# Moments of nine chunks made early, the experts' square moved to ScalarE, and one tile map made in two parts, in a perceiver block on one core

## The reference, cut to what matters

```python
x = x + xattn(layernorm(x), ctx_1024, ...)       # 64 sequences of 32 tokens, 257 context rows each, D = 256
# x + attn(layernorm(x), ...): time mixing, then a mixture of 8 experts
probs = jax.nn.softmax(ei @ router_w, axis=-1)
vals, idx = jax.lax.top_k(probs, 2)
tw = jnp.sum(jax.nn.one_hot(idx, E) * (vals / vals.sum(-1, keepdims=True))[..., None], axis=-2)
k_e = jnp.square(jax.nn.relu(jnp.einsum('ebsd,edf->ebsf', xk_e, eWk)))   # F = 512
kv_e = jnp.einsum('ebsf,efd->ebsd', k_e, eWv)
r_e = jax.nn.sigmoid(jnp.einsum('ebsd,edg->ebsg', xr_e, eWr))
moe = jnp.einsum('ebsd,bse->bsd', r_e * kv_e, tw)
# x + ffn(layernorm(x), ...): a shared GEGLU and one of 8 GEGLU experts for each token
```

## Time and profile before

| | |
|---|---|
| median of 3 runs | 944.83 us (944.8 to 945.19) |
| the profiled execution | 948.37 us, span 946.3 us |
| PE busy | 863.0 us, 91% of the span |
| DVE busy | 457.3 us, 48% |
| ACT busy | 316.4 us, 33% |
| POOL busy | 342.7 us, 36% |

### The profile page before, as it was taken

How to read it: one execution, slowest core, us unless ns; L and a number is a source line. 1 busy time by engine, 2 the same in 40 slices (tenths; PEclk the granted TensorE clock), 3 DMA queues, 4 the chain that set the end, 5 groups by cost and what they waited for, 6 DMA issues and landing times.

```text
span 946.3 us, 18950 instructions
## 1 busy us (share of the span) xinstructions
PE 863.0 (91%) x6360; PEld 774.4 (82%) x6360; DVE 457.3 (48%) x1355; ACT 316.4 (33%) x714; POOL 342.7 (36%) x580
## 2 busy tenths in 40 slices
PE   5899988887767789999967999999999999999998
PEld 4567767665666679999957999999999999999998
DVE  1269988889873565555535666621111111111114
ACT  1366767665453334444421111111111111111110
POOL 1444677775876336654313333010001100000033
PEclk9899999998589889999997999999999999999999
DMA  9775457435512222253311122065898989998114
GB/s 353 262 265 211 162 161 246 124 118 207 167 40 63 52 63 84 82 174 126 79 42 54 57 67 68 12 245 207 322 318 304 308 325 318 306 323 288 56 52 134
DMA packets 92110, 162.00 MB, mean 171 GB/s; under 512 B 13832, under 2 KB 71112, under 8 KB 88680
## 3 DMA queue, kind: packets, MB, share of 16 engines
q1 hardware_dynamic: 71008, 103.39, 32.6%
q10 hardware_dynamic: 12832, 37.82, 10.6%
q0 software_dynamic: 8176, 19.57, 7.8%
HBM read 146.10 MB, written 14.66 MB: 170 GB/s over the span
## 4 chain that ended last, share of the span: by engine, by line
PE 65%; DVE 13%; POOL 6%; DVEq 6%; issue 5%; DMA 3%; ACT 1%; ACTq 1%; another core or an unknown queue 0%; SPq 0%; POOLq 0%
PE bank L1635 27%; PE bank L1648 14%; PE bank L372 7%; PE bank L399 7%; PE bank L386 3%; DMA xz<-in_x_dram 2%; DVEq L1388 2%; PE bank L361 1%; DVE arena_b L1191 1%; POOL tab_e L685 1%; PE bank L779 1%; DVE arena_b L1211 1%; DMA arena_a<-rows_y,slot 1%; PE bank L1618 1%; DVE arena_b L501 0%
## 5 line engine op out<-in xcount | busy, mean ns | idle before, releaser
L1635 PEld LDWEIGHTS bank<-arena_b,arena_a 128*128 128x128 f32 x1472 | 168.0, 192 | 1.2
L1635 PE MATMUL bank<-arena_b,arena_a 128*128 128x128 f32 x1472 | 168.1, 275 | 0.0
L1701 ACT ACTIVATE arena_b<-bank 128x512 f32<-128x512 f32 x78 | 46.6, 597 | 301.0 <-PE bank L1635 301.0
L1843 DVE TENSOR_TENSOR arena_b<-bank,arena_b 128x512 f32<-128x512 f32 x78 | 54.0, 692 | 190.8 <-PE bank L1635 186.0
L1635 PE MATMUL bank<-arena_b,a_x 128*128 128x128 f32 x1024 | 122.6, 280 | 0.0
L1635 PEld LDWEIGHTS bank<-arena_b,a_x 128*128 128x128 f32 x1024 | 119.6, 196 | 0.4
L328 POOL DMA_INDIRECT arena_a<-rows_e,pick x78 | 76.0, 975 | 29.5 <-issue 29.5
L372 PE MATMUL bank<-arena_b,arena_a 128*128 128x128 f32 x624 | 82.2, 289 | 4.2 <-DVE hT L509 4.2
L1648 PE MATMUL bank<-arena_a,arena_b 128*128 128x256 f32 x368 | 83.2, 379 | 0.0
L372 PEld LDWEIGHTS bank<-arena_b,arena_a 128*128 128x128 f32 x624 | 78.6, 205 | 5.0 <-DVE arena_b L501 2.9
L1539 POOL COPY pick<-list_i 128x1 uint32 x23 | 4.2, 182 | 206.6 <-PE bank L1618 180.5
(11 more groups left out here) (275 smaller groups left out, 1365.8 us busy)
## 6 DMA issues: line engine op xcount, KB each, us to landing
arena_a<-in_W_dram SPq DMA_DIRECT2D x69, 1024.0 KB
arena_a<-in_ctx_n_dram ACTq DMA_DIRECT2D x16, 1152.0 KB
arena_a<-in_ctx_t_dram SPq DMA_DIRECT2D x16, 1028.0 KB
rows_y<-arena_a ACTq DMA_DIRECT2D x39, 128.0 KB
arena_a<-in_w_moe_dram ACTq DMA_DIRECT2D x3, 1156.0 KB
arena_a<-in_w_moe_dram ACTq DMA_DIRECT2D x3, 1152.0 KB
rows_f<-arena_b ACTq DMA_DIRECT2D x23, 128.0 KB
rows_e<-arena_b SPq DMA_DIRECT2D x64, 32.0 KB
```

The costliest lines, as they stand in the source:

```text
L1635: last = nc.tensor.matmul(bank[half][:, f * P:(f + 1) * P], w12[:, i, k, col0:col0 + P], zT[:, k], start=k == 0, stop=k == KD - 1)
L1701: nc.scalar.activation(act_g[:, half], bU[half][:], ACT.Gelu).then_inc(g_ac_g, 1)
L1843: nc.vector.tensor_tensor(hT_f[:, u % 2, half * HH:(half + 1) * HH].rearrange("p f t -> p (f t)"), bG[half][:], act_g[:, half], ALU.mult). ...
```

## The change

Three edits.

1. `stats0` and `moments0` of chunks 3 to 11 leave the beginning of steps 2 to 10. Chunk 3 is now done at the end of step 1, chunks 4 and 5 at the end of step 2, 6 to 8 at the end of step 3, 9 to 11 at the end of step 4, each group with one drain between its statistics and its moments. `mv0` holds all 16 chunks, `st0` four.
2. DVE's product `squared` (128x512, bank times relu) is gone. ACT squares its own relu output right after the relu, ahead of the sigmoid, and waits for its own relu in between. `hidden(n)` now waits for the relu of tile `n - 1`.
3. `tile_map` becomes `tile_counts`, behind step 24 and with it behind DVE's mixture step 5, and `tile_map`, behind DVE's mixture step 6.

```diff
--- before.py
+++ after.py
@@ -119,7 +119,7 @@
         zero_rows = sb("zero_rows", [BATCH, D])
         w_tab = sb("w_tab", [P, KD, P])
         rs_2 = sb("rs_2", [P, G])
-        st0, mv0, rs0 = (sb(n, [P, 2, w]) for n, w in (("st0", 6), ("mv0", 2), ("rs0", 3)))
+        st0, mv0, rs0 = sb("st0", [P, 4, 6]), sb("mv0", [P, G, 2]), sb("rs0", [P, 2, 3])
         st1, mv1, rs1 = (sb(n, [P, 2, w]) for n, w in (("st1", 6), ("mv1", 2), ("rs1", 5)))
         smx, snm, srec = (sb(n, [P, 2, 1]) for n in ("smx", "snm", "srec"))
         ssum = sb("ssum", [P, 3, 1])
@@ -259,7 +259,7 @@
             "po_set po_num po_r3 po_ei po_sum po_tab")
 
         m_pa, m_pr, m_ph, m_py, m_ap, m_asig, m_arelu, m_awk = sems1("m_pa m_pr m_ph m_py m_ap m_asig m_arelu m_awk")
-        m_dd, m_dx, m_dsq, m_dy, m_mu, m_gap = sems1("m_dd m_dx m_dsq m_dy m_mu m_gap")
+        m_dd, m_dx, m_asq, m_dy, m_mu, m_gap = sems1("m_dd m_dx m_asq m_dy m_mu m_gap")
         m_got = [sem1(f"m_got{i}") for i in range(NM)]
         m_put = [sem1(f"m_put{i}") for i in range(NM)]
         m_x12, dv_map_a, dv_cnt_a, pe_tot_a, po_tab_a = sems1("m_x12 dv_map_a dv_cnt_a pe_tot_a po_tab_a")
@@ -366,7 +366,7 @@
                 pe.wait_ge(m_awk, n + 1)
                 if n == 0:
                     pe.wait_ge(ac_er, G)
-                need(pe, m_dsq, n)
+                need(pe, m_arelu, n)
                 for f in range(FKC):
                     for k in range(KD):
                         last = nc.tensor.matmul(bMH[:, f * P:(f + 1) * P],
@@ -393,7 +393,7 @@
                     pe.wait_ge(dv_ev, G)
                     pe.wait_ge(ld_moe_k, 16 * 4)
                     pe.wait_ge(ld_moe_v, 16 * 3)
-                pe.wait_ge(m_dsq, n + 1)
+                pe.wait_ge(m_asq, n + 1)
                 need(pe, m_dy, n)
                 for f in range(FKC):
                     last = nc.tensor.matmul(bMY[:, 0:D], hT[:, n % 2, f * P:(f + 1) * P],
@@ -427,8 +427,10 @@
 
             def units(n):
                 act.wait_ge(m_ph, n + 1)
-                need(act, m_dsq, n - 1)
                 nc.scalar.activation(h_relu[:, n % 2], bMH[:], ACT.Relu).then_inc(m_arelu, 1)
+                need(act, m_py, n - 1)
+                act.wait_ge(m_arelu, n + 1)
+                nc.scalar.activation(hT[:, n % 2], h_relu[:, n % 2], ACT.Square).then_inc(m_asq, 1)
                 act.wait_ge(m_pr, n + 1)
                 need(act, m_dy, n - 1)
                 nc.scalar.activation(sig[:, n % 2], bMR[:, 0:D], ACT.Sigmoid).then_inc(m_asig, 1)
@@ -503,11 +505,6 @@
                                                               ALU.mult, ALU.add)
                 last.then_inc(m_dx, 1)
 
-            def squared(n):
-                dve.wait_ge(m_arelu, n + 1)
-                need(dve, m_py, n - 1)
-                nc.vector.tensor_tensor(hT[:, n % 2], bMH[:], h_relu[:, n % 2], ALU.mult).then_inc(m_dsq, 1)
-
             def gated(n):
                 dve.wait_ge(m_py, n + 1)
                 dve.wait_ge(m_asig, n + 1)
@@ -517,8 +514,6 @@
             def step(m):
                 if m < NT1:
                     mixed(m)
-                if 0 <= m - 1 < NT1:
-                    squared(m - 1)
                 if 0 <= m - 2 < NT1:
                     gated(m - 2)
                 if m == TA:
@@ -623,11 +618,11 @@
                 r = rs0[:, n % 2]
                 pool.wait_ge(dv_st0, n + 1)
                 need(pool, ac_hn, n - 1)
-                nc.gpsimd.tensor_scalar(r[:, 0:1], mv0[:, n % 2, 1:2], EPS, None, ALU.add).then_inc(po_r0, 1)
+                nc.gpsimd.tensor_scalar(r[:, 0:1], mv0[:, n, 1:2], EPS, None, ALU.add).then_inc(po_r0, 1)
                 pool.wait_ge(po_r0, 3 * n + 1)
                 nc.gpsimd.tensor_tensor(r[:, 1:2], r[:, 0:1], eps_pow[:], ALU.pow).then_inc(po_r0, 1)
                 pool.wait_ge(po_r0, 3 * n + 2)
-                nc.gpsimd.tensor_scalar(r[:, 2:3], mv0[:, n % 2, 0:1], -1.0, r[:, 1:2], ALU.mult, ALU.mult).then_inc(po_r0, 1)
+                nc.gpsimd.tensor_scalar(r[:, 2:3], mv0[:, n, 0:1], -1.0, r[:, 1:2], ALU.mult, ALU.mult).then_inc(po_r0, 1)
 
             def rstd1(n):
                 v, r = mv1[:, n % 2, 1:2], rs1[:, n % 2]
@@ -1139,10 +1134,10 @@
             def stats0(n):
                 part = [i for i, (lo, hi) in enumerate(X_PARTS) if lo <= n < hi][0]
                 dve.wait_ge(ld_x[part], 16)
-                nc.vector.bn_stats(st0[:, n % 2], xz[:, n])
+                nc.vector.bn_stats(st0[:, n % 4], xz[:, n])
 
             def moments0(n):
-                nc.vector.bn_aggr(mv0[:, n % 2], st0[:, n % 2]).then_inc(dv_st0, 1)
+                nc.vector.bn_aggr(mv0[:, n], st0[:, n % 4]).then_inc(dv_st0, 1)
 
             def own_value(n):
                 dve.wait_ge(pe_v, n + 1)
@@ -1303,8 +1298,7 @@
                 nc.vector.tensor_tensor(place1[:, 0:TA], te_f[:, 0:TA], tb_f[:, 0:TA], ALU.subtract).then_inc(dv_map_a, 1)
 
 
-            def tile_map():
-                left = NT1 - TA
+            def tile_counts():
                 dve.wait_ge(pe_tot, 1)
                 nc.vector.tensor_tensor(cmp_eg, bK[:, 0:E].unsqueeze(2).to_broadcast([P, E, G]),
                                         tile_lo[:].unsqueeze(1).to_broadcast([P, E, G]), ALU.is_gt)
@@ -1315,6 +1309,9 @@
                 nc.vector.tensor_tensor(n_tiles[:], n_tiles[:], taken_a[:, 0:E], ALU.subtract)
                 dve.drain()
                 nc.vector.tensor_tensor_scan(t_end[:], ones_e[:], n_tiles[:], 0.0, ALU.mult, ALU.add)
+
+            def tile_map():
+                left = NT1 - TA
                 dve.drain()
                 nc.vector.tensor_tensor(cmp_te[:, 0:left], t_end[:].unsqueeze(1).to_broadcast([P, left, E]),
                                         iota_t[:, 0:left].unsqueeze(2).to_broadcast([P, left, E]), ALU.is_le)
@@ -1342,8 +1339,11 @@
                 nc.vector.scalar_tensor_tensor(w, lora_bank[i][:], LORA_SCALE, w, ALU.mult, ALU.add).then_inc(dv_set, 1)
             dve.wait_ge(ld_e, 16)
             moe = moe_vector(dve)
+            AHEAD = (3, 4, 6, 9, 12)
             for s in range(STEPS):
                 a, b, c, t = live(s), live(s - 1), live(s - 2), live(s + 1)
+                if 2 <= s < AHEAD[-1] - 1:
+                    t = None
                 z, k, w, x, h = (live(s - LAG - i) for i in (0, 1, 2, 3, 5))
                 if w is not None:
                     decayed(w)
@@ -1417,12 +1417,19 @@
                     tile_map_a()
                 if a is not None:
                     largest_score(a)
-                if s == STEPS - 1:
-                    tile_map()
+                if 1 <= s < len(AHEAD):
+                    for n in range(AHEAD[s - 1], AHEAD[s]):
+                        stats0(n)
+                    dve.drain()
+                    for n in range(AHEAD[s - 1], AHEAD[s]):
+                        moments0(n)
                 if s >= MOE_AT:
                     moe(s - MOE_AT)
+            tile_counts()
             for m in range(STEPS - MOE_AT, MSTEPS):
                 moe(m)
+                if m == STEPS - MOE_AT:
+                    tile_map()
```

## The result

The changed kernel took **936.61 us** (median of 4 runs, 933.93 to 937.09) against 945.01 for the kernel before beside it: ratio **0.9905, 95% interval 0.9886 to 0.9924**, faster by about 1%. The profiled execution took 936.4 us, with a span of 934.7. In two later comparisons the same kernel came to 936.52 and 935.31 (ratios 0.9925 and 0.9903).

A forecast was written before the change was run, and what follows sets the result against it. PE was taken to bound the kernel, busy nine tenths, its idle stretches being what edits could gain. The sum -8.4 + 0.7 - 0.6 - 0.8 = -9.1 us from the 944.83 median gave 935.7 us, range 933 to 940.5.

The forecast's parts named there:

- The main case: Whole kernel: 935.7 us, the map's stall behind the totals gone, a small wait at tile 9 new; chance 0.73.
- The 0.6 behind the row numbers: Behind `row_numbers`, `hidden(10)` no longer waits for the square but for mixtures ending earlier: 0.6 us gained.
- the 0.8 for the moments: Steps 5 to 9, paced by DVE: late by 1.0 us in step 5, early by step 9, 0.8 us gained.
- Map and square: 8.4 forecast: Totals to `turned(7)`: 4.86 us in place of 13.26; 8.4 gained as 4.2 waiting, 1.3 square, 2.9 slow clock.
- The forecast's 1.3 for the square: At `hidden(5)` behind the totals: PE's wait for DVE's square of tile 4 goes, 1.3 us of the 8.4.
- The two rivals in which the clock or the mixtures hold PE up: Behind the totals: clock stays low near 310 us, 938.5 (chance 0.08); or late mixtures hold `turned(7)`, 943 (0.04).
- The wait at tile 9: 0.7 forecast: At `turned(9)`: the later map delays lists and gathers, so PE newly waits 0.7 us, bounds 0 to 2.
- The rival that wanted 2 us more: At `turned(9)`: lists and gathers take 2 us more, PE waits 2.7, L372 slows by 2.8: 940.5; chance 0.12.
- the word "unchanged" on the 2.62: Behind `row_numbers` at 343.13: PE's wait of 2.62 us, with DVE busy 6.5 us, was said to stay.
- The 0.9 us for unexplained waits: Ahead of the totals, around 300 us: if waits the profile can't name belong to every run, up to 0.9 more gained.
- The rival with tables (1010 us): Mixture tiles: square and sigmoid in different tables, two 1.28 us loads a tile, 73 us slower, about 1010; chance 0.03.
- Its second estimate, 120 us more: Same tables rival by the skill page's 2.66 us a switch: 5.3 us a tile, about 120 us more.

The follow-up runs named there:

- g_moments_map: The changed kernel with the square put back on DVE (early moments and the map in two parts kept): 935.66 us, ratio 0.9908 to the kernel before.
- f_map_sooner: The changed kernel with the rest of the map moved between tile 6's mixtures and `gated(4)`: 932.97 us, ratio 0.9897 to the kernel before.

## Why the prediction was right, point by point

- **The sum.** 935.7 was forecast, 936.61 measured, in the range and within 0.1% of it. The main case came true in its mechanism: the map's stall went, and a small wait at tile 9 came. That the number is so close is partly luck. The 0.6 behind the row numbers and the 0.8 for the moments did not come, the stretch from the totals to `turned(12)` differs by 1.5 us between traces of the same changed kernel (37.25, 35.79, 36.34), and most of the gain ahead of the totals belongs to no edit.
- **Map and square: 8.4 forecast, 8.55 in the trace.** It belongs to the map alone: g_moments_map has the square on DVE and the same 4.88. The forecast's 1.3 for the square is a real wait in the trace of before, but it came from the order of the map, which stood ahead of the square too. The square on ACT is worth nothing that can be measured, alone (0.9996) or beside the map (940.45 against 940.05, 935.31 against 935.66). The two rivals in which the clock or the mixtures hold PE up are refuted by L372 at 1.95 us and `turned(7)` at 4.88.
- **The wait at tile 9: 0.7 forecast, 1.17 measured,** 1.33 with what the step lost besides. The mechanism and the place were right. The hops were 0.73, 2.02, 1.91 and 3.23 us for 0.7, 1.7, 2.0 and 2.9: list and gather were 0.3 slower each than the rows of before. The place is also confirmed by f_map_sooner, in which the map ends 2.1 us sooner and the wait is gone. The rival that wanted 2 us more, and with them a slow L372, did not come: behind 1.17 us L372 took 1.95.
- **Behind the row numbers: 0.6 forecast.** `hidden(10)` starts 1.22 us after `turned(11)`, before 1.91, which is 0.69. But the wait ahead of it grew from 2.62 to 2.95, and L399 behind it took 2.27 us in place of 1.89, so that only 0.27 arrives at `turned(12)`, and -0.11 with the 0.38 lost ahead. One step that failed is the word "unchanged" on the 2.62. The rows show where DVE was later: `row_numbers` took 6.92 us in place of 6.59, for in the middle of it DVE stood still, and what for the profile doesn't name:

```profile
327.23 0.17 DVE L478 TENSOR_TENSOR moved_a<-moved_a,moved 128x8 f32<-128x8 f32 x1 [0.41 <-issue]
```

  The term is also too small to see: from `turned(9)` to `turned(12)` three traces of the changed kernel take 21.41, 20.01 and 20.71 us, before 21.30, and g_moments_map, with the square on DVE, 20.25.
- **The moments: 0.8 forecast, and this term is wrong in kind.** Step 5 was late by 0.66 us where 1.0 was said, and by the end of step 7 DVE was 0.47 early. The step that failed is that steps 8 and 9 would go on gaining 0.4 each: they lost 0.35 each. The loop through ACT's logits, which the forecast has from step 9 on, would explain it one step early, and DVE waits 0.43 us for them in step 8; that is argued and not tested. Alone the edit measures 1.0002. The forecast's own bound (0.6 lost to 1.2 gained) holds that.
- **The 0.9 us for unexplained waits.** They come and go under one program, and cost PE two waits of together 3.2 us in the trace of before. That would fit the profiled execution of before (948.37), which stood 3.5 us above its median, and the two spans, which differ by 11.6 where the medians differ by 8.4; the other executions have no trace, so it isn't shown. The sum against the trace (939.3) was 2.9 us above the profiled execution of the change, the sum against the median 0.9 below its median: taking the median was the better choice.
- **ACT.** Three table loads as before, squares of 0.63 us each behind relus of 0.60; steady tiles at 120 of 120 us. The rival with tables (1010 us) is refuted. Its second estimate, 120 us more, doesn't come out of its terms: 5.3 in place of 2.6 us in each of 39 tiles is 105 us more than the 73, 179 in all. The groups by line of the kernel after, with one of the three loads:

```profile
L433 ACT ACTIVATE hT<-h_relu 128x512 f32<-128x512 f32 x39 | 24.6, 630 | 3.5
L444 ACT ACT_TABLE_LOAD x1 | 1.3, 1283 | 0.0
```

The page "ScalarE: Activation LUTs" of the Trainium skill, section "What ACT_TABLE_LOAD costs", gives by its price of 186 ns and 0.833 ns a column an estimated 0.61 us for this square; the trace has 0.63. The rule in its section "Rules for kernel authors", VectorE and not ScalarE for mul and relu, would have kept the square on DVE: the move measures 0.9996 alone, neither good nor bad, and in the steady tiles PE is busy for 120 of 120 us with the square on either engine.

## What to carry to other kernels

A block of small operations on an engine that is half idle can still stop the engine that is full: look at what stands directly behind the block, put the successor's inputs ahead of it, and cut the block to the slack of one step (six pieces in place of one gave 5.3 us in the stretch concerned). Behind the row numbers the pause of the matrix engine cost half as much again as it lasted, in slow matmuls (5.3 us for 3.6). And before a gain of a few us is put down to an edit, run the same program twice, and set the stretch where the edit works beside the median: two traces of one program differed by 3.7 us in one step, and the same wait for the square that one trace showed was absent from another kernel with the same order.
